# Normalized rows turned in squares by VectorE and moved by transfers, with the first pass's weight splits two chunks earlier, in a macaron block on one core

## The chip, the cores and the metric

The kernel runs on 1 core of a Trainium2 chip (trn2). The metric is the device time of one execution in microseconds (us). A matmul unit (TensorE, PE in the rows), VectorE (DVE), ScalarE (ACT) and GpSimd (POOL) each work through a list of instructions in order. SyncE (SP) only issues transfers; ScalarE and GpSimd issue some of theirs. PEld is TensorE's load of the stationary operand.

## The reference, cut to what matters

The input is 2 x 1024 tokens of 512 float32 values. Three layers follow one another, each on normalized rows:

```python
x = x + 0.5 * ffn(layernorm(x))
x = x + attention(layernorm(x))
x = x + 0.5 * ffn(layernorm(x))
```

with, for each token of `ffn` (8 groups of 352 hidden values, 64 router columns, 8 chosen):

```python
scores = softmax(x @ gate_w.T); w = top-8 of scores, scattered into 64 columns
flat = w[inv_map]; scalar = flat.sum(-1); soft = softmax(where(flat == 0, -1e9, flat))
xg = x + soft @ mask_up_w                        # for each group
y = sum over groups of scalar * (silu(xg @ Wg.T) * (xg @ Wu.T)) @ Wd.T
```

and `attention` a gated linear attention with 4 heads of 128 (keys) and 64 (values), worked in chunks of 64 tokens: projections to q, k, v, a decay and a gate, a state carried from chunk to chunk, a norm of each head's output, the gate, and a product with Wo.

## The kernel before

Four blocks of 512 tokens go through eight **phases** (p = 0 to 7). Each phase is one feed-forward layer of one block: 22 **chunks** (c), each of 128 of the 2816 hidden values. Phases 1, 2, 4 and 5 hold in addition the attention of a block (`ATT`). Every product in high precision is three TensorE products (`three`): each operand is split into a rounded part (`_hi`) and the rest (`_lo`), and `hi*hi`, `lo*hi` and `hi*lo` are added up. A split is one ScalarE copy that rounds and one VectorE subtraction.

TensorE's list for a chunk is: the gate half `main(GB)` (12 matmuls and one of `soft`), the up half `main(UB)` (12 and one), then `down` of the chunk before (12). Between these stand three **slots** per chunk, `pieces(3n)`, `pieces(3n + 1)` and `pieces(3n + 2)`, numbered k = 0 to 65 within a phase. In them all engines do, in the same numbering, what is not feed-forward matmul: `attention(t, k, q)` of this phase and `router(p, k)` for the next phase. VectorE runs slot 3n + 1 between `gate` (two products that make `act_t`) and `rest_a` (which makes `a_lo`), and slots 3n + 2 and 3n + 3 after `rest_a`; ScalarE runs slots 3n and 3n + 1 between `silu` and `round_a`, and slot 3n + 2 after it.

Before its product with weights a normalized row must lie with its features on the partitions. There are 12 normalizations of 512 rows: one for each phase's router (`LN_R`) and one for each attention (`LN_T`). Each has four tiles of 128 tokens. For a tile, VectorE writes `xn` (`norm`, line 728), TensorE turns it with four 128 x 128 transposes (`turn`, line 1063) into a bank, ScalarE rounds the bank into `x_hi` (`hi`), and VectorE writes the rest to `x_lo` (`low`). The tiles of a router sit in slots 32, 33, 35 and 36 (chunks 10 to 12), those of an attention in 7, 8, 10 and 11 (chunks 2 and 3). The router's product with `gate_s` is slot 38 (lines 1083 and 1084); the attention's first product is slot 13. `W0` and `W1` are the two banks that the slots share.

The weights of a chunk (`wt`, 1152 KB, line 272, and `dt`, 512 KB, line 281) are loaded by SP in order, `load_w(p, c)` and then `load_d(p, c - 1)`, into one of two halves. `load_w` of chunk c waits until the up half of chunk c - 2 is done (`u_ok`) and is needed by `main(GB)` of chunk c.

In phase 0 (the **first pass**) the weights arrive unsplit. ScalarE's `gu_hi(c + 1)` and VectorE's `gu_lo(c + 1)` split those of the next chunk at the head of chunk c, ahead of `silu` and `gate`; TensorE's `masked(c + 1)` (lines 1251 and 1252) behind the up half of chunk c needs them.

Of the kernel before, what the change touches and what calls it, by code (L numbers as in the profile page):

```python
# [33 lines left out]
NCK = NB // CK  # L34
EPS = 1e-5
# [27 lines left out]
def build(nc, x, wgu, wdn, wat, w_gate, w_mup, w_gk1, w_gk2, bgk, wnorm, inv, c_id, c_mask, c_reset, c_iota, c_rank, out):  # L63
    with ExitStack() as ctx:
# [14 lines left out]
        x_hi = sb("x_hi", [P, 2, KC, NB], F32R)  # L79
        x_lo = sb("x_lo", [P, 2, KC, NB], F32R)  # L80
        softT = sb("softT", [P, 2, 2, NB], F32R)
        s_bc = sb("s_bc", [P, 2, NB])
        a_hi = sb("a_hi", [P, 2, NB], F32R)
        a_lo = sb("a_lo", [P, 2, NB], F32R)
# [56 lines left out]
        xn = o_all[:].rearrange("p (a b) c -> p a (b c)", a=2)  # L141
        tb_flat = tb[:].rearrange("p a b -> p (a b)")
# [6 lines left out]
        zmin, spl = tb[:, 0:4, :], b_all  # L149

# [10 lines left out]
        def first_w(c):  # L161
# [27 lines left out]
        stats_ok, mv_ok, ve_ok, rstd_ok, xn_ok, xT_ok, x_hi_ok, x_lo_ok = (  # L189
            sem(n) for n in ("stats_ok", "mv_ok", "ve_ok", "rstd_ok", "xn_ok", "xT_ok", "x_hi_ok", "x_lo_ok"))  # L190
# [30 lines left out]
        def tr_bank(p, i):  # L221
            return YB[i] if p == 0 else W1
# [29 lines left out]
        def _(sp):  # L252
# [29 lines left out]

            for i in range(NT):
                sp.dma_start(xr(0)[:, i, :], x_t[0][:, i, :]).then_inc(ld_x0[i], 16)
# [5 lines left out]
            raw_gate_up(2)  # L290
            for c in range(2, CH):
# [126 lines left out]
        def _(act):  # L418
# [17 lines left out]
            def t_hi(t, s):  # L436
# [11 lines left out]
                elif s == S_VG:  # L448
                    act.wait_ge(k_mm, t * H)
# [10 lines left out]
            def hi(r, i, s, b):  # L460
                act.wait_ge(xT_ok, r * NT + i + 1)
                copy(x_hi[:, s, :, cols(i)], b[:].rearrange("p (k c) -> p k c", k=KC)).then_inc(x_hi_ok, 1)

            def router(p, k):
                r = LN_R[p]
                if k in (32, 33, 35, 36):
                    i = (32, 33, 35, 36).index(k)
                    if i == 0 and p:

                        wait(act, u_ok, (p - 1) * CH)  # L470
                        if p - 1 in ATT:
                            act.wait_ge(k_mm, (ATT[p - 1] + 1) * H)
                    hi(r, i, p % 2, tr_bank(p, i))
# [35 lines left out]
            def attention(t, k, q):  # L509
# [57 lines left out]
                if k in (40, 46, 52, 58):  # L567
                    h = (k - 40) // 6
                    act.wait_ge(o_ok, t * H + h + 1)
                    if h == 0:  # L570

                        act.wait_ge(xT_ok, (LN_R[q + 1] + 1) * NT)
# [3 lines left out]
                elif k in (61, 62, 63, 64):  # L576
                    i = k - 61
                    act.wait_ge(ogT_ok, t * NT + i + 1)
                    wait(act, wo_ok, t * NT + i - 1)
                    copy(og[:, i % 2, 0, :, :], W1[:, 0:2 * P].rearrange("p (v c) -> p v c", v=2)).then_inc(og_hi_ok, 1)  # L580
# [39 lines left out]
            router(0, 32)  # L620
            router(0, 33)
            act.wait_ge(ld_gate, 16)
            copy(gate_s[:, :, 0:E], raw_gate).then_inc(gate_hi_ok, 1)
            router(0, 35)
            router(0, 36)
# [14 lines left out]
            gu_hi(2)  # L640
            router(0, 45)
# [9 lines left out]
            for p in range(PHASES):  # L651
                for c in range(CH):
                    n = p * CH + c
                    if p == 0 and 1 < c < CH - 1:
                        gu_hi(c + 1)
# [12 lines left out]
                    if p == 0:  # L668
                        d_hi(c)
                    pieces(3 * n + 2)  # L670

        @block.vector
        def _(dve):
# [50 lines left out]
            def norm(r, i, src):  # L724
                dve.wait_ge(mv_ok, r * NT + i + 1)
                dve.wait_ge(rstd_ok, r * NT + i + 1)
                wait(dve, xT_ok, r * NT + i - 1)
# [3 lines left out]
            def low(r, i, s, b):  # L731
                dve.wait_ge(x_hi_ok, r * NT + i + 1)
                tt(x_lo[:, s, :, cols(i)], b[:].rearrange("p (k c) -> p k c", k=KC),
                   x_hi[:, s, :, cols(i)].bitcast(F32), ALU.subtract).then_inc(x_lo_ok, 1)

            def router(p, k):
# [5 lines left out]
                if k == 28:  # L742
# [6 lines left out]
                elif k == 29:  # L749
                    stats_of(r, 2, src)  # L750
                    stats_of(r, 3, src)
                elif k == 31:
                    norm(r, 0, src)
                    norm(r, 1, src)
                elif k in (32, 33, 35, 36):
                    i = (32, 33, 35, 36).index(k)
                    low(r, i, p % 2, tr_bank(p, i))
                    if i < 2:
                        norm(r, i + 2, src)
# [103 lines left out]
            def attention(t, k, q):  # L863
# [7 lines left out]
                elif k == 5:  # L871

                    wait(dve, ogT_ok, t * NT)
                    norm(r, 0, xb)
                    norm(r, 1, xb)
                elif k in (7, 8, 10, 11):
                    i = (7, 8, 10, 11).index(k)
                    low(r, i, s, (W0, W1)[i % 2])
                    if i < 2:
                        norm(r, i + 2, xb)  # L880
# [42 lines left out]
                if k in (61, 62, 63, 64):  # L923
                    i = k - 61
# [469 lines left out]
```

## Time and profile before

| | |
|---|---|
| median of 3 runs | 1871.08 us (1869.36 to 1872.04) |
| the profiled execution's own time | 1871.53 us |
| its span, first to last instruction | 1869.8 us |
| busy: TensorE, VectorE, ScalarE, GpSimd | 99%, 45%, 28%, 8% |
| mean granted TensorE clock | 0.995 |

The profile shows one execution. Its own time is 1.7 us above its span, and 0.45 us above the median. TensorE is busy nearly throughout; what it does and where it stops are read in the order of time, since a transfer or VectorE can hold it only in some places.

### The profile page before, as it was taken

The page shows a single profiled execution, that of the slowest core. Times are in us where ns is not written, and L with a number is a line of the kernel's source. Part 1 is how long each engine was busy: PE and PEld are TensorE (multiplying, and loading weights), DVE is VectorE, ACT ScalarE, POOL GpSimd, SP SyncE. Part 2 cuts the span into 40 slices and gives each one's busy share as a digit, 9 for nine tenths or more (in the row PEclk, how much of TensorE's full clock was granted, in tenths as well). Part 3 has the DMA queues.
Part 4 walks back from the last instruction along what each step waited for, and adds up shares of the span by engine and source line. Part 5 has one row for each costly group of instructions (what it writes and reads, how often), then busy time and mean ns, then how long its engine had stood idle before and what let it go on. Part 6 is the DMA issues. An engine that isn't in the chain of part 4 may idle for free.

```text
span 1869.8 us, 22348 instructions
## 1 busy us (share of the span) xinstructions
PE 1843.0 (99%) x8608; PEld 1533.7 (82%) x8608; DVE 841.2 (45%) x1599; ACT 526.4 (28%) x802; POOL 141.3 (8%) x246
## 2 busy tenths in 40 slices
PE   7998999999999999999999999999999999999999
PEld 5887888888888888888888888888888888888887
DVE  7455553646344554323433556353654323422222
ACT  3333422533124432111211533123532111311111
POOL 1131110010000100000010010000000000000000
PEclk9998999999999999999999999999999999999999
DMA  5985855545464455376655555455445466656664
GB/s 196 345 290 192 302 191 174 189 152 183 147 212 159 149 178 201 109 255 231 211 173 194 189 190 173 163 186 174 149 174 183 135 234 214 211 165 247 217 237 172
DMA packets 90345, 366.83 MB, mean 196 GB/s; under 512 B 11680, under 2 KB 12064, under 8 KB 69504
## 3 DMA queue, kind: packets, MB, share of 16 engines
q1 hardware_dynamic: 50064, 262.89, 40.5%
q10 hardware_dynamic: 27792, 47.20, 9.5%
q0 software_dynamic: 12384, 55.32, 7.5%
q8 instruction: 69, 1.13, 0.3%
q14 instruction: 36, 0.29, 0.0%
HBM read 323.55 MB, written 41.81 MB: 195 GB/s over the span
## 4 chain that ended last, share of the span: by engine, by line
PE 94%; DVE 3%; ACT 1%; issue 1%; DMA 1%; SPq 0%; POOL 0%; DVEq 0%; ACTq 0%
PE bank L1053 27%; PE bank L1055 27%; PE bank L1054 27%; PE bank L1266 4%; PE bank L1063 1%; PE bank L1207 1%; PE bank L1199 1%; PE bank L1206 1%; PE bank L1251 1%; PE bank L1193 1%; PE bank L1252 1%; PE bank L1083 0%; PE bank L1084 0%; PE bank L1091 0%; DMA x_res<-x 0%
## 5 line engine op out<-in xcount | busy, mean ns | idle before, releaser
L1053 PE MATMUL bank<-x_hi,wt 128*128 128x512 f32 x1328 | 524.1, 395 | 0.0
L1055 PE MATMUL bank<-x_lo,wt 128*128 128x512 f32 x1328 | 517.8, 390 | 0.0
L1054 PE MATMUL bank<-x_hi,wt 128*128 128x512 f32 x1328 | 516.9, 389 | 0.0
L675 DVE TENSOR_TENSOR act_t<-bank,sig 128x512 f32<-128x512 f32 x176 | 121.6, 691 | 571.9 <-PE bank L1266 511.7
L1055 PEld LDWEIGHTS bank<-x_lo,wt 128*128 128x128 f32 x1328 | 249.2, 188 | 53.2
L1054 PEld LDWEIGHTS bank<-x_hi,wt 128*128 128x128 f32 x1328 | 249.6, 188 | 50.2
L1053 PEld LDWEIGHTS bank<-x_hi,wt 128*128 128x128 f32 x1328 | 249.5, 188 | 49.5
L1053 PE MATMUL bank<-dt,a_hi 128*128 128x512 f32 x704 | 280.1, 398 | 0.3 <-DVE a_lo L675 0.3
L1055 PE MATMUL bank<-dt,a_hi 128*128 128x512 f32 x704 | 275.8, 392 | 0.0
L1054 PE MATMUL bank<-dt,a_lo 128*128 128x512 f32 x704 | 275.3, 391 | 0.0
L600 ACT ACTIVATE sig<-bank 128x512 f32<-128x512 f32 x176 | 105.5, 600 | 526.7 <-PE bank L1266 526.6
L420 ACT ACTIVATE a_hi<-act_t 128x512 fp32r<-128x512 f32 x176 | 111.1, 631 | 356.8 <-DVE act_t L675 349.3
L675 DVE TENSOR_TENSOR a_lo<-act_t,a_hi 128x512 fp32r<-128x512 f32 x176 | 121.4, 690 | 125.7 <-ACT a_hi L420 125.2
L1055 PEld LDWEIGHTS bank<-dt,a_hi 128*128 128x128 f32 x704 | 132.7, 188 | 28.8
L1053 PEld LDWEIGHTS bank<-dt,a_hi 128*128 128x128 f32 x704 | 133.2, 189 | 26.5 <-issue 0.7
L1054 PEld LDWEIGHTS bank<-dt,a_lo 128*128 128x128 f32 x704 | 133.0, 189 | 25.9
L1266 PE MATMUL bank<-softT,wt 128*128 128x512 f32 x352 | 134.5, 393 | 1.0 <-ACT softT L420 1.0
L675 DVE TENSOR_TENSOR act_t<-s_bc,act_t 128x512 f32<-128x512 f32 x176 | 129.2, 734 | 6.7 <-DMA s_bc<-scr_s 0.8
L1053 PE MATMUL bank<-x_hi,tw 128*128 128x512 f32 x208 | 81.6, 392 | 0.0
L1054 PE MATMUL bank<-x_hi,tw 128*128 128x512 f32 x208 | 81.4, 391 | 0.0
L1055 PE MATMUL bank<-x_lo,tw 128*128 128x512 f32 x208 | 81.3, 391 | 0.0
L1266 PEld LDWEIGHTS bank<-softT,wt 128*128 128x128 f32 x352 | 66.5, 189 | 15.0 <-issue 1.2
(178 smaller groups left out, 1690.9 us busy)
## 6 DMA issues: line engine op xcount, KB each, us to landing
wt<-scr_w SPq DMA_DIRECT2D x140, 1152.0 KB, 5.2
dt<-scr_d SPq DMA_DIRECT2D x140, 512.0 KB, 5.3
s_bc<-scr_s ACTq DMA_DIRECT2D x128, 256.0 KB, 5.2
state<-wat POOLq DMA_DIRECT2D x28, 512.0 KB, 6.2
scr_w<-wt POOLq DMA_DIRECT2D x12, 1024.0 KB, 7.6
b_all<-wgu SPq DMA_DIRECT2D x22, 512.0 KB, 6.7
scr_d<-dt POOLq DMA_DIRECT2D x22, 512.0 KB, 4.7
scr_w<-tw POOLq DMA_DIRECT2D x10, 1024.0 KB, 7.8
```

The costliest lines, as they stand in the source:

```text
L420: return nc.scalar.activation(dst, src, ACT.Copy)
L600: nc.scalar.activation(sig[:], g_bank(n)[:], ACT.Silu).then_inc(sig_ok, 1)
L675: return nc.vector.tensor_tensor(dst, a, b, op)
L1053: mm(dst, wh, xh, start=start, stop=False)
L1054: mm(dst, wl, xh, start=False, stop=False)
L1055: return mm(dst, wh, xl, start=False, stop=stop)
L1063: ins = nc.tensor.transpose(b[:, cols(k)], xn[:, i % 2, cols(k)], ident[:])
L1193: ins = mm(W0[:, cols(i)], b_all[:, h, cols(i)], q_all[:, h, cols(i)], start=True, stop=True)
L1199: ins = mm(W0[:, cols(i)], k2t[:, i, :], vtz[:, i, h, :, :], start=True, stop=True)
L1206: mm(W0[:, cols(i)], scm[:, h % 2, i, :], vtz[:, i, h, :, :], start=True, stop=False)
L1207: ins = mm(W0[:, cols(i)], q_all[:, h, cols(i)], state[:, h % 2, 2 * i:2 * i + 2, :], start=False, stop=True)
L1266: return mm(b[:], m[:, c0:c0 + P], softT[:, p % 2, c % 2, :], start=False, stop=True)
```

## The change

**Turning.** Except for the first normalization, TensorE no longer turns normalized rows. VectorE's `turn_squares` turns a tile in 32 x 32 squares into `squares` (space in `tb`), one instruction of 128 x 512. When four tiles are done (`sq_ok`), SP's `move_squares` moves them with 16 transfers of 32 partitions x 2 KB (64 KB each) into the space of `x_lo`. ScalarE then rounds two halves of 128 x 1024 into `x_hi` and VectorE writes the rests over `x_lo` (`hi`, `low`, two each in place of four). `move_squares` stands in SP's list after `load_d(p, 2)` for an attention and after `load_d(p, 11)` for a router, ahead of the next `load_w`.

**Order of tokens.** A tile of the residual holds 32 tokens of each quarter of the block, so `x_hi`, `x_lo`, `a_hi` and `a_lo` get further dimensions; TensorE's moving operand of 512 columns becomes four runs of 128, and the host reorders the rows of the input and the output.

**Slots.** The router's statistics are in 27 and 28, its norms and turns in 30 and 31 (31 and 32 where the phase holds an attention), the splits in 36 and 37. The attention's norms and turns are in 5 and 6, the splits in 10 and 11. The transposes of the gated heads (slots 61 to 64, one tile each) are done two tiles at a time in 61 and 63, and the products with Wo two tiles at a time in 64 and 65.

**First pass.** `gu_hi(c + 3)` and `gu_lo(c + 3)` stand behind the split of the down weights at the end of chunk c; chunk 3's are split before the loop.

```diff
+            def move_squares(r, s):
+                sp.wait_ge(sq_ok, r * NT)
+                for b in range(NQ):
+                    for j in range(NQ):
+                        sp.dma_start(turned(s)[cols(j, Q), b, :, :, :], squares[cols(b, Q), j, :, :, :]).then_inc(sq_in[b // 2], 16)
...
-                if c + 1 < CH:
-                    raw_gate_up(c + 1)
+                if c + 2 < CH:
+                    raw_gate_up(c + 2)
+                if c == 13:
+                    move_squares(LN_R[1], 1)
                 raw_down(c)
...
+                    if c == 3 and p in ATT:
+                        move_squares(LN_T[ATT[p]], (p + 1) % 2)
+                    if c == 12 and p + 1 < PHASES:
+                        move_squares(LN_R[p + 1], (p + 1) % 2)
...
+            def hi(r, m, s):
+                act.wait_ge(sq_in[m], 16 * 2 * NQ * r)
+                b = slice(2 * m, 2 * m + 2)
+                copy(x_hi[:, s, b, :, :, :], turned(s)[:, b, :, :, :]).then_inc(x_hi_ok, 2)
...
-                if k in (7, 8, 10, 11):
-                    i = (7, 8, 10, 11).index(k)
-                    if i == 0:
-                        act.wait_ge(u_ok, q * CH)
-                    hi(r, i, s, (W0, W1)[i % 2])
+                if k in (10, 11):
+                    hi(r, k - 10, s)
...
-                copy(a_hi[:, n % 2, :], act_t[:]).then_inc(a_hi_ok, 1)
+                copy(by_quarter(a_hi[:, n % 2, :, :, :]), in_order(act_t[:])).then_inc(a_hi_ok, 1)
...
-                    if p == 0 and 1 < c < CH - 1:
-                        gu_hi(c + 1)
                     silu(n)
...
                         d_hi(c)
+                        if 0 < c < CH - 3:
+                            gu_hi(c + 3)
...
+            def turn_squares(r, i):
+                dve.wait_ge(xn_ok, r * NT + i + 1)
+                nc.vector.transpose(squares[:, :, :, i, :].rearrange("p j k t -> p k j t"),
+                                    xn[:, i % 2, :].rearrange("p (k j t) -> p k j t", k=KC, j=NQ)).then_inc(sq_ok, 1)
...
+            def low(r, m, s):
+                dve.wait_ge(x_hi_ok, r * NT + 2 * m + 2)
+                b = slice(2 * m, 2 * m + 2)
+                tt(x_lo[:, s, b, :, :, :], turned(s)[:, b, :, :, :], x_hi[:, s, b, :, :, :].bitcast(F32),
+                   ALU.subtract).then_inc(x_lo_ok, 2)
...
+                if k in (norm_slot(p), norm_slot(p) + 1):
+                    i = 2 * (k - norm_slot(p))
...
+                    for j in (i, i + 1):
+                        norm(r, j, src)
+                        turn_squares(r, j)
+                elif k in (36, 37):
+                    low(r, k - 36, p % 2)
...
+            def xk(s, k):
+                return tuple(x[:, s, :, k, :, :].rearrange("p b i t -> p b (i t)") for x in (x_hi, x_lo))
...
-                    turn(r, i, tr_bank(p, i))
```

## Rows read from the trace of the kernel before

**Rows 1.** The page: busy us of each engine, share of the span, instructions.

```profile
PE 1843.0 (99%) x8608; PEld 1533.7 (82%) x8608; DVE 841.2 (45%) x1599; ACT 526.4 (28%) x802; POOL 141.3 (8%) x246
```

**Rows 2.** Waits of TensorE: us in total, times, longest us.

```profile
PE bank L1063 <- DVE o_all L728: 10.3, 6, 6.7
PE bank L1251 <- DVE wt L675: 6.1, 2, 3.3
PE bank L1251 <- DVE tw L675: 2.2, 2, 1.4
```

**Rows 3.** Timeline of SP: start us, us; issues of `load_w` and `load_d`.

```profile
529.06 0.32 SPq L281 DMA_DIRECT2D dt<-scr_d  x1
...
534.95 0.32 SPq L272 DMA_DIRECT2D wt<-scr_w  x1
...
544.54 0.32 SPq L272 DMA_DIRECT2D wt<-scr_w  x1
...
800.39 0.32 SPq L272 DMA_DIRECT2D wt<-scr_w  x1
...
809.00 0.32 SPq L272 DMA_DIRECT2D wt<-scr_w  x1
```

**Rows 4.** The chain that ended last, phase 1, chunk 10: a turn.

```profile
393.66 0.44 PE bank L1063 x4
```

**Rows 5.** Windows of the first pass: busy us by engine, granted clock, DMA share.

```profile
142.70:149.00 6.30, 6.30 (x20) 5.34 (x21) 3.37 (x6) 1.68 (x3) 1.60 (x3) 0.53 0.85 286
...
159.00:162.20 3.20, 3.19 (x12) 2.90 (x13) 2.30 (x5) 1.22 (x3) 1.07 (x2) 0.50 0.62 175
```

**Rows 6.** Timeline of the first pass, chunk 11: VectorE, TensorE.

```profile
140.37 0.69 DVE L675 TENSOR_TENSOR x_lo<-bank,x_hi 128x512 fp32r<-128x512 f32 x1 [5.47 <-ACT x_hi L420]
...
141.43 1.22 DVE L675 TENSOR_TENSOR wt<-b_all,wt 128x1024 fp32r<-128x1024 f32 x1
...
142.70 0.58 PE L1251 MATMUL bank<-wt,og 128*128 128x256 f32 x1 [3.26 <-DVE wt L675]
```

**Rows 7.** Groups by form, VectorE: busy us, mean ns of one.

```profile
L728 DVE TENSOR_SCALAR o_all<-x_res,mv,rstd 128x512 f32<-128x512 f32 x44 | 22.9, 540 | 0.1
...
L675 DVE TENSOR_TENSOR x_lo<-bank,x_hi 128x512 fp32r<-128x512 f32 x48 | 33.1, 689 | 58.4 <-ACT x_hi L420 58.4
...
L675 DVE TENSOR_TENSOR tw<-state,tw 128x1024 fp32r<-128x1024 f32 x28 | 34.2, 1220 | 30.8 <-ACT tw L420 30.8
```

**Rows 8.** Timeline of phase 2, chunks 1 to 4: VectorE, TensorE.

```profile
529.42 1.00 DVE L728 TENSOR_SCALAR o_all<-x_res,mv,rstd 128x512 f32<-128x512 f32 x2
...
547.91 0.48 PE L1053 MATMUL bank<-x_hi,wt 128*128 128x512 f32 x1
```

**Rows 9.** Timeline of SP and of ScalarE's queue: runs of issues.

```profile
0.80 1.81 SPq L284 DMA_DIRECT2D x_res<-x  x4
...
1698.26 0.80 ACTq L595 DMA_DIRECT2D s_bc<-scr_s  x2
...
536.42 2.54 ACTq L595 DMA_DIRECT2D s_bc<-scr_s  x2
```

**Rows 10.** Transfers by line: count, KB each, median us from issue to landing.

```profile
wt<-scr_w SPq DMA_DIRECT2D x140, 1152.0 KB, 5.2
...
s_bc<-scr_s ACTq DMA_DIRECT2D x32, 64.0 KB, 5.0
...
out<-x_res SPq DMA_DIRECT2D x4, 256.0 KB, 2.1
```

**Rows 11.** Timeline of phase 1, chunks 10 to 12: VectorE, ScalarE, TensorE.

```profile
388.47 1.00 DVE L728 TENSOR_SCALAR o_all<-x_res,mv,rstd 128x512 f32<-128x512 f32 x2
...
389.16 0.63 PE L1063 MATMUL bank<-ident,o_all 128*128 128x128 f32 x4 [0.46 <-DVE o_all L728]
...
403.28 0.60 ACT L600 ACTIVATE sig<-bank 128x512 f32<-128x512 f32 x1 [2.40 <-PE bank L1266]
...
411.41 0.48 PE L1083 MATMUL bank<-x_hi,gate_s 128*128 128x512 f32 x1
```

More of the change, by code:

```diff
@@ L219, in xr, with turned, by_quarter, in_order @@
             return x_res[:, b % 3, :, :]
-        def tr_bank(p, i):
-            return YB[i] if p == 0 else W1
+        def turned(s):
+            return x_lo[:, s, :, :, :, :].bitcast(F32)
+        def by_quarter(a):
+            return a.rearrange("p i b t -> p b i t")
+        def in_order(a):
+            return a.rearrange("p (b i t) -> p b i t", b=NQ, i=NT)
+        def norm_slot(p):
+            return 31 if p - 1 in ATT else 30
         def router_src(p):
@@ L871, in attention @@
                 elif k == 5:
[L873 to L880, printed above, removed]
+                    wait(dve, ogT_ok, 2 * t)
+                    dve.wait_ge(u_ok, q * CH)
+                    dve.wait_ge(routeT_ok, 2 * (q + 1))
+                if k in (5, 6):
+                    for i in (2 * k - 10, 2 * k - 9):
+                        norm(r, i, xb)
+                        turn_squares(r, i)
+                if k in (10, 11):
+                    low(r, k - 10, s)
                 if k in (13, 14, 15, 16):
@@ L1022, in _ @@
             gu_lo(2)
+            gu_lo(3)
             for p in range(PHASES):
@@ L1025, in _ @@
                     n = p * CH + c
-                    if p == 0 and 1 < c < CH - 1:
-                        gu_lo(c + 1)
                     gate(n)
@@ L1042, in _ @@
                         d_lo(c)
+                        if 0 < c < CH - 3:
+                            gu_lo(c + 3)
                     pieces(3 * n + 2)
@@ L1055, in three, with xtile, first_turn @@
                 return mm(dst, wh, xl, start=False, stop=stop)
-            def xk(s, k, c=slice(0, NB)):
-                return x_hi[:, s, k, c], x_lo[:, s, k, c]
-            def turn(r, i, b):
-                pe.wait_ge(xn_ok, r * NT + i + 1)
+            def xk(s, k):
+                return tuple(x[:, s, :, k, :, :].rearrange("p b i t -> p b (i t)") for x in (x_hi, x_lo))
+            def xtile(s, k, b):
+                return tuple(x[:, s, b, k, :, :].rearrange("p i t -> p (i t)") for x in (x_hi, x_lo))
+            def first_turn(i):
+                pe.wait_ge(xn_ok, i + 1)
                 for k in range(KC):
-                    ins = nc.tensor.transpose(b[:, cols(k)], xn[:, i % 2, cols(k)], ident[:])
+                    ins = nc.tensor.transpose(YB[i][:, cols(k)], xn[:, i % 2, cols(k)], ident[:])
                 ins.then_inc(xT_ok, 1)
@@ L1150, in attention @@
                     for kk in range(KC):
-                        mm(W1[:], k1_s[:, kk, :], x_hi[:, s, kk, :], start=(kk == 0), stop=False)
-                        ins = mm(W1[:], k1_s[:, kk, :], x_lo[:, s, kk, :], start=False, stop=(kk == KC - 1))
+                        x_h, x_l = xk(s, kk)
+                        mm(W1[:], k1_s[:, kk, :], x_h, start=(kk == 0), stop=False)
+                        ins = mm(W1[:], k1_s[:, kk, :], x_l, start=False, stop=(kk == KC - 1))
                     ins.then_inc(z1_ok, 1)
@@ L1223, in attention @@
-                if k in (61, 62, 63, 64):
-                    i = k - 61
+                        pe.wait_ge(t_lo_ok, t * SLABS + S_WO + 1)
+                    for i in (2 * k - 128, 2 * k - 127):
+                        if i > 1:
+                            pe.wait_ge(x2_ok, t * NT + i - 1)
+                        w = tw[:, (t * SLABS + S_WO) % 2, :].rearrange("p (a v c) -> p a v c", a=2, v=2)
+                        for v in range(2):
+                            g = [ogT(t)[:, m, v, i, :, :].rearrange("p b t -> p (b t)") for m in range(2)]
+                            ins = three((W0, W1)[i % 2][:], g, (w[:, 0, v, :], w[:, 1, v, :]), v == 0, v == 1)
+                        ins.then_inc(wo_ok, 1)
@@ L1285, in down @@
                 for t in range(NT):
-                    ins = three(YB[t][:], (a_hi[:, n % 2, cols(t)], a_lo[:, n % 2, cols(t)]), (w[:, 0:D], w[:, D:2 * D]), i == 0, i == CH - 1)
+                    ins = three(YB[t][:], tuple(a[:, n % 2, t, :, :].rearrange("p b t -> p (b t)") for a in (a_hi, a_lo)), (w[:, 0:D], w[:, D:2 * D]), i == 0, i == CH - 1)
                     if i == CH - 1 and t + 1 < NT:
@@ L1291, in _ @@
             pe.wait_ge(ld_id, 16)
-            for k in range(32, 37):
-                router(0, k)
+            for i in range(NT):
+                first_turn(i)
             pe.wait_ge(gate_ok, 1)
```

181 lines of the change are left out of this document (84 added, 97 removed).

## The prediction

> **What bounds the kernel now.** I read the page first: TensorE is busy for 1843.0 of 1869.8 us [rows 1], so only two things shorten the kernel, work taken off TensorE and its stops. The work in question is 192 transposes of normalized rows (12 normalizations of 16), of which the first 16 stay. The waits show its stops [rows 2]: on the norm before a transpose (6 times; the longest, 6.7 us, is the start of the kernel and stays) and on the split weights of the first pass (4 times, 8.3 us). The timelines give the prices, and what stands ahead of what.
>
> **Transposes off TensorE: -20.9 us.** 11 normalizations x 4 tiles x 4 = 176 transposes go, 44 turns of four. A busy sum misprices them, since they overlap and the matmul behind starts late; I price by distances. Two chunks of phase 3 without a turn are 8.61 us apart, and two of phase 2 with two turns between them 9.59 [rows 3]: 0.49 us for a turn. In the chain the turns in the chunks beside the attention's own small products take 0.44 [rows 4]. So 28 turns (16 of attentions, 12 of routers outside attention phases) at 0.49 and 16 at 0.45: 13.7 + 7.2 = 20.9 (19.4 to 21.6 by one price for all).
>
> **The wait before one turn of each attention phase: -2.6 us.** In phase 1 TensorE idles 0.46 us for the norm ahead of the turn at 389.16, which then itself takes 0.63 [rows 11]; less the 0.44 counted above this is 0.65 us, and the other attention phases repeat it: four times: -2.6.
>
> **First pass: -13.3 us.** In chunk 11 VectorE's `x_lo` waits for ScalarE's `x_hi`, which stands behind `silu`; `gu_lo`, which TensorE needs, stands behind it on VectorE, and TensorE stops for 3.26 us [rows 6]. The next chunk repeats it. After the change the splits stand at the end of a chunk and are needed over two chunks later, so nothing of 10 us can reach TensorE: the 8.3 us of [rows 2] go, with some 0.5 for the restarts. After each of the two long stops the granted clock is 0.53 over 6.3 us and 0.50 over 3.2, against 1.00 around [rows 5], that is the level of 1.2 GHz for 6.3 x 0.94 + 3.2 = 9.1 us, in which half as much was done: 4.5 us come back. Together 13.3. The cover is two chunks, over 17 us; if it went, all 13 would return. Chunk 3's split, moved before the loop, takes 1.2 us on VectorE where it waited for the first `s_bc`: nothing.
>
> **What VectorE gets.** A turn of 128 x 512 is not in this trace. From below it costs what the norm costs, 0.54 us; from above twice the sum that reads a bank, or as much as 1024 columns, 1.22 [rows 7]. I take 0.66, near the other one-pass instructions of 512 columns (0.54 to 0.69). With the norm (0.57 with its hand-over) a tile is 1.16 to 1.2 us, four 4.8. Two splits of 1024 (1.22 each) replace four of 0.69: -0.3. VectorE has over half its time free, so only places matter. The Trainium skill, page "VectorE: DVE Perf Modes", section "The three transpose paths", gives 311 ns for 128 columns in two-byte data, and says that only 32 x 32 blocks are turned; four of these would be an estimate of 1.24 us, the upper end here, and put the sum at the third rival's. No row of this trace shows the instruction.
>
> **SP's queue, attention: +1.3 us each.** Here the change adds a wait with something behind it. VectorE starts the norms of an attention at 529.42 [rows 8]; with 4.8 us and 0.1 for the signal SP is released at 534.3. Then 16 issues. Four plain issues took 1.81 us, 0.45 each; two for part of the partitions 0.80; in a busy moment two took 2.54 [rows 9]. I take 0.48, 7.7 us, to 542.0. Behind them stands `load_w(4)`, which was issued at 534.95 [rows 3]. Landing 5.2 us later [rows 10], it is there at 547.3. TensorE started that chunk at 547.91 [rows 8] behind four turns that are now gone (-1.96): it wants it at 546.0. So it stops for 1.3 us, 5.2 in four phases. At 0.40 for an issue it would not stop. The bounds: 0 to 5.6 (a turn of 1.22 adds 2.2, issues of 0.61 add 2.1).
>
> **Router in an attention phase: +0.2 us each.** The norms start at 388.47 [rows 11]; with `rest_a` between the two slots the squares are ready at 394.0, issued by 401.7, landed by 403.8 to 406.7 (2.1 to 5.0 us [rows 10]). `silu` of chunk 12 was at 403.28 [rows 11] and comes 2.0 earlier (the wait of 0.65 and three turns); ScalarE's second split stands behind the copies of the attention's scores in slot 37, by my estimate 406.4 to 407.5, and VectorE's rest ends at 408.8. TensorE wants slot 38 at 411.41 less 2.5 (a fourth turn), 408.9. It stops for 0.2, with landings late 1.5: 0.8 us in four phases. `load_w(13)`, issued at 401.7, lands at 406.9 and is wanted at 410.9. Outside attention phases the squares are ready two chunks early; the two splits around `gate` leave slot 38 about 0.1 us late, three times: 0.3.
>
> **At nothing.** The tail of the attention: with two tiles, ScalarE's and VectorE's two operations each of 256 columns (under 0.69 [rows 7]) need, by my estimate, 2.3 us behind slot 63, and TensorE's up half covers 13 x 8.61 / 38 = 2.95 [rows 3]. The runs of 32 in `a_hi` and the four runs of 128 in the moving operand: the trace has no such matmul, its runs of 128 in VectorE's writes cost no more (0.69 [rows 7]); a nanosecond for each of 6000 would be 6 us.
>
> **Sum.** -20.9 - 2.6 - 13.3 = -36.8; +5.2 + 0.8 + 0.3 = +6.3; -30.5. Against the profiled execution's own 1871.5 that is 1841.0, and the median of the runs stands 0.45 lower: 1840.6, **1841**.
>
> **Rivals.**
> 1. Nothing stops TensorE: issues of 0.40 or less. Then 1871.1 - 36.8 + 1.1 = 1835. For it speaks that transfers within the memory are short; against it that the plainest run was at 0.45. Chance 0.14.
> 2. The first pass keeps its stops, at another place (raw weights or stores late, now that TensorE is faster): 1841 + 13 = 1854. Its DMA share is 0.85 after the stop [rows 5]. Chance 0.05.
> 3. The turn costs 1.22 us. SP is released 2.2 us later, the stop at the start of an attention is 3.5 us, long enough for the lower clock as after the stops of 3 us in the first pass [rows 5] (1.5 more), and slot 38 is about 1 us late: 4 x 6 = 24 in place of 6.3, 1859. Chance 0.12.
> 4. The other side: SP's issues back up. One ScalarE run took 2.54 for two [rows 9]. If each of the 16 took 0.95 us, `load_w(4)` would be issued 7.5 us later still: a stop of 8.8 and 1.5 for the clock, and slot 38 and `load_w(13)` 3 to 5 us late, 4 x 14 = 56 against 36.8: 1890. It decides from about 0.75 us for an issue. Against it: the squares are ready 5.2 us after `load_d(2)` was issued at 529.06 [rows 3], when the queue should be empty. Chance 0.07. The Trainium skill, page "DMA: Bandwidth & Descriptors", section "Bandwidth", has 64 KB transfers at 0.95 us, bound by their descriptors; one behind another they would give this rival's time. The rows here have no transfer between two places in the core's memory.
> 5. The moving operand in four runs slows each matmul by a few ns: 2 ns x 6000 = 12 us, 1853; from 5 ns there is no gain. No row speaks for it. Chance 0.05.
>
> **How the numbers follow.** The forecast keeps 0.57, with its own range of 1836 to 1849 (the stop of an attention at 0 to 3 us). 8 in 10 is reached from 1834 to 1858, which takes in rivals 1, 2 and part of 5 and touches 3. Faster by over 0.2% (3.7 us, about what a measurement of this kernel tells from no change) is all but rival 4 and half of 5: 0.90; within it 0.03; slower 0.07.
>
> **What the profile after would show.** Right: 16 transposes in line `turn`'s place and TensorE 8432 matmuls; no wait of TensorE on split weights and a clock of 1.00 to 256 us; the VectorE turn near 0.66 us; 176 issues of 64 KB near 0.48; four waits of `main(GB)` of chunk 4 on `wt`, 1.3 us each; chunks of 8.61 us where there were turns. Wrong: waits of 3 us or more at chunk 4 or slot 38, matmuls further apart than 0.227 us, or stops in the first pass.

## The result, and the profile after

The change makes the kernel slower: 1887.62 us median (1886.73 to 1887.87, 4 runs) against 1871.56 for the kernel before beside it, a ratio of 1.0086 [1.0069, 1.0104]. The forecast was 1841, so 46.6 us have to be explained. The forecast named the side that came true, rival 4, at a chance of 0.07.

The page after, its totals, then the group of the squares among its transfers:

```profile
PE 1828.4 (97%) x8432; PEld 1520.0 (81%) x8432; DVE 872.1 (46%) x1621; ACT 521.4 (28%) x780; POOL 142.3 (8%) x246
...
PE 86%; DVE 5%; SPq 4%; DMA 3%; issue 1%; ACT 1%; POOL 0%; DVEq 0%; ACTq 0%
...
x_lo<-tb SPq DMA_DIRECT2D x176, 64.0 KB, 2.4
```

Against [rows 1] TensorE has 176 instructions less and 14.6 us less busy time, in a span 15.1 us longer: it stands still for longer. The second line is the share of each engine in the chain that ended last; SP's queue and the transfers now hold 7% of it, where they held 1% before.

Waits of TensorE, which answer to [rows 2] (us in total, times, longest):

```profile
PE bank L1111 <- DMA wt<-scr_w: 33.2, 5, 8.6
PE bank L1124 <- DVE o_all L764: 8.4, 2, 6.7
PE bank L1140 <- DVE x_lo L710: 7.7, 3, 5.8
```

The waits on split weights are gone, and those on the norm are at the start of the kernel only. New are five waits on `wt`, a load that SP issues, and one of 5.8 us for `x_lo` at slot 38. Four of the five on `wt` stand at chunk 4 of an attention phase: 6.8, 8.5, 6.8 and 8.6 us. The one of phase 2, on TensorE's and SP's timelines (start, us):

```profile
542.32 0.39 PE L1113 MATMUL bank<-dt,a_hi 128*128 128x512 f32 x1
551.19 0.79 PE L1111 MATMUL bank<-x_hi,wt 128*128 128x512 f32 x1 [8.48 <-DMA wt<-scr_w]
...
531.18 10.02 SPq L313 DMA_DIRECT2D x_lo<-tb  x16
541.24 0.58 SPq L298 DMA_DIRECT2D wt<-scr_w  x1
541.87 0.57 SPq L307 DMA_DIRECT2D dt<-scr_d  x1
542.48 0.43 SPq L298 DMA_DIRECT2D wt<-scr_w  x1
542.96 1.58 SPq L307 DMA_DIRECT2D dt<-scr_d  x1
```

The 16 issues take 10.02 us, 0.63 each. SP ran idle up to 531.18, waiting for the squares. `load_w(4)` goes out only at 541.24, and TensorE had nothing left to do at 542.7. Four loads then leave within 1.7 us, where [rows 3] has the two `load_w` among them 9.6 us apart. `load_w(4)` landed in 9.9 us; the row of that one issue, in the kernel after and, for the same chunk, in the kernel before:

```profile
wt<-scr_w SPq DMA_DIRECT2D x1, 1152.0 KB, 9.9
```

```profile
wt<-scr_w SPq DMA_DIRECT2D x1, 1152.0 KB, 7.8
```

The second line was there to be read before the change. The forecast took the median of 140 loads, 5.2 [rows 10], for a load that already took 7.8. Phase 2 is the worst of four: in phases 1, 2, 4 and 5 `load_w(4)` landed in 7.2, 9.9, 6.7 and 9.4 us, 8.3 on the mean, against 6.8, 7.8, 7.8 and 7.3 before the change, 7.4 on the mean.

What follows a stop, in windows of the kernel after (busy us of PE, PEld, DVE, ACT, POOL; then the granted clock, the DMA share, GB/s):

```profile
551.20:554.20 3.00, 3.00 (x7) 2.42 (x8) 0.00 (x0) 0.00 (x0) 0.00 (x0) 0.50 0.89 365
554.20:557.20 3.00, 3.00 (x13) 2.44 (x13) 0.00 (x0) 0.60 (x1) 0.00 (x0) 0.93 0.16 62
```

TensorE had been still for 8.5 us and worked the next 3.4 us at the level of 1.2 GHz: 1.5 us more in the first window, and 0.2 in the one behind. The same holds for all six stops that are new with the change (five on `wt`, and slot 38 below): the work at the low level behind them lasted 2.9 to 5.3 us, 21.5 in all. In the first pass SP's queue looks worse still, and slot 38 waits for it:

```profile
135.31 16.48 SPq L313 DMA_DIRECT2D x_lo<-tb  x16
151.83 0.58 SPq L287 DMA_DIRECT2D k_all<-wdn  x1
...
155.82 0.77 PE L1140 MATMUL bank<-x_hi,gate_s 128*128 128x512 f32 x1 [5.84 <-DVE x_lo L710]
```

So the 46.6 us, from these rows: the waits on `wt` at chunk 4 of four phases are 33.2 - 2.6 = 30.6 us (the fifth, 2.6, is `load_w(13)` of phase 4), 25.4 more than the 5.2 foreseen; the fifth 2.6; slot 38 of the first pass 5.8; the low clock behind the six stops 10.7, an estimate from 1.7 for the 3.4 us of phase 2. The 1.1 foreseen at slot 38 outside the first pass came to 0.3: -0.8. Together 43.7. Of the 2.9 us that are left, the first pass's own gain, which the first experiment finds 2.0 short of the forecast, can be the larger part; the rest I cannot place.

### The profile page after: what moved, and what is told of

Its sections match the earlier page's. It is cut to its first block, busy times and chain, and to the rows that moved or that the text cites. A ratio compares the mean times of both kernels' runs of the same rounds, so it can differ in the third digit from the quotient of the medians.

```text
span 1884.9 us, 22151 instructions
## 1 busy us (share of the span) xinstructions
PE 1828.4 (97%) x8432; PEld 1520.0 (81%) x8432; DVE 872.1 (46%) x1621; ACT 521.4 (28%) x780; POOL 142.3 (8%) x246
## 4 chain that ended last, share of the span: by engine, by line
PE 86%; DVE 5%; SPq 4%; DMA 3%; issue 1%; ACT 1%; POOL 0%; DVEq 0%; ACTq 0%
PE bank L1111 25%; PE bank L1113 25%; PE bank L1112 25%; SPq L313 4%; PE bank L1317 4%; DMA wt<-scr_w 2%; DVE tb L769 1%; PE bank L1257 1%; PE bank L1256 1%; DVE o_all L764 1%; PE bank L1243 1%; PE bank L1249 1%; DVE act_t L710 1%; PE bank L1140 1%; PE bank L1302 0%
## 5 line engine op out<-in xcount | busy, mean ns | idle before, releaser
L1111 PE MATMUL bank<-x_hi,wt 128*128 128x512 f32 x1328 | 526.2, 396 | 33.2 <-DMA wt<-scr_w 33.2
L1317 PEld LDWEIGHTS bank<-softT,wt 128*128 128x128 f32 x352 | 66.7, 190 | 15.1 <-issue 1.2
```

The source lines that it names most:

```text
L1111: mm(dst, wh, xh, start=start, stop=False)
L1317: return mm(b[:], m[:, c0:c0 + P], softT[:, p % 2, c % 2, :], start=False, stop=True)
```

## The experiments

All kernels were timed beside the kernel before. The reading at the start: 16 issues in series on SP, ahead of a weight load, cost the time (theory). Against it stood the bytes, and VectorE's turn.

**The first pass alone.** The kernel before, with the splits of the first pass moved and nothing else.

```diff
+            raw_gate_up(3)
...
-                if c + 1 < CH:
-                    raw_gate_up(c + 1)
+                if c + 2 < CH:
+                    raw_gate_up(c + 2)
...
+                        if 0 < c < CH - 3:
+                            gu_hi(c + 3)
```

> The kernel before with one part of the change alone: the first pass splits its gate and up weights three chunks ahead. TensorE turns the rows as before. The prediction priced this part at -13.3 us. Theory (this part kept its promise and the loss lies in the squares): 1858 us, 1855 to 1861, and no stop of TensorE for a split weight in chunks 11 to 15 of the first pass. Rival (the first pass keeps stops, its gain is small): 1866 or more.

Measured: 1860.0 us (1859.3 to 1860.5), ratio 0.9939 [0.9921, 0.9957]. Against the kernel before beside it this is -11.3 of the -13.3. The waits of TensorE hold no split weight any more; the norm and the start are left:

```profile
PE bank L1066 <- DVE o_all L730: 10.7, 7, 6.6
PE bank L1111 <- DVE tb L811: 2.0, 1, 2.0
PE bank L1086 <- DVE x_lo L677: 1.5, 1, 1.5
```

This term of the sum kept its promise within 2 us. The loss lies in the squares.

**Loads ahead of squares.**

```diff
                     if c > 1:
                         load_w(p, c)
+                    if c == 4 and p in ATT:
+                        move_squares(LN_T[ATT[p]], (p + 1) % 2)
+                    if c == 13 and p in ATT:
+                        move_squares(LN_R[p + 1], (p + 1) % 2)
                     if c > 2:
                         load_d(p, c - 1)
-                    if c == 3 and p in ATT:
-                        move_squares(LN_T[ATT[p]], (p + 1) % 2)
-                    if c == 12 and p + 1 < PHASES:
+                    if c == 12 and p + 1 < PHASES and p not in ATT:
                         move_squares(LN_R[p + 1], (p + 1) % 2)
```

> The changed kernel with the 16 square transfers of the attention phases issued by SP behind load_w(4) and ahead of load_d(3), and those of the router in the same phases behind load_w(13). Nothing else is moved, and the same bytes move. Theory (16 issues of 0.63 us stand ahead of load_w(4) on SP's queue, and the loads behind them go out in a bunch): the four stops of 6.9 to 8.75 us at chunk 4 go with the lower clock behind them, and the load of chunk 13 of phase 4 comes in time: 1887.6 - 31 - 6 - 3 = about 1848 us, 1843 to 1855; the stop of 6 us in the first pass stays. Rival 1 (the squares' bytes hold up the weights, whatever the order of issue): 1875 or more. Rival 2 (VectorE's turn comes late): no change, 1887.

Measured: 1855.59 us (1852.7 to 1858.6), 0.9915 [0.9894, 0.9937]. The same transfers in another order are worth 32 us, and turn the loss into a gain. It came out just above the theory's upper edge, because the squares, in turn, come late. Waits of TensorE:

```profile
PE bank L1142 <- DVE x_lo L712: 13.4, 6, 5.8
PE bank L1126 <- DVE o_all L766: 8.3, 3, 6.5
PE bank L1113 <- DVE x_lo L712: 3.3, 3, 2.0
```

No wait on `wt` is left. Of the 13.4 us at slot 38, 1.5 are the kernel's start, 5.8 the first pass and 6.2 the four attention phases; 3.3 are the attention's first product.

**Two issues in the place of sixteen.**

```diff
-                for b in range(NQ):
-                    for j in range(NQ):
-                        sp.dma_start(turned(s)[cols(j, Q), b, :, :, :], squares[cols(b, Q), j, :, :, :]).then_inc(sq_in[b // 2], 16)
+                for m in range(2):
+                    h = slice(2 * m, 2 * m + 2)
+                    sp.dma_start(turned(s)[:, h, :, :, :], squares[:, h, :, :, :]).then_inc(sq_in[m], 16)
```

> The changed kernel with the squares moved by 2 transfers of 128 partitions and 512 KB in the place of 16 of 64 KB. It leaves out the exchange between blocks of 32 partitions, so the rows are not in order; the bytes, the place on SP's queue and all that waits are the same. Theory (the number of issues is what costs): all stops at chunk 4 and the one of 6 us in the first pass go, 1836 us, 1832 to 1843, which is near the forecast's rival without stops. Rival 1 (the bytes on the DMA engines hold up the weights): the second half of each stop, about 4.7 of 8.6 us, stays: four of those with the lower clock behind them are 20 to 25 us, 1857 to 1862. Rival 2 (VectorE's turn comes late): 1887.

Measured: 1837.31 us (1836.9 to 1837.7), 0.9818 [0.98, 0.9835]. The bytes and the place in the queue are those of the change, and 50.3 us are gone. Its waits of TensorE, then SP's timeline at chunk 4 of phase 2:

```profile
PE bank L1124 <- DVE o_all L764: 8.9, 3, 6.6
PE bank L1140 <- DVE x_lo L710: 3.4, 2, 1.9
```

```profile
516.99 1.16 SPq L313 DMA_DIRECT2D x_lo<-tb  x2
518.19 0.92 SPq L298 DMA_DIRECT2D wt<-scr_w  x1
519.94 0.33 SPq L307 DMA_DIRECT2D dt<-scr_d  x1
```

`load_w(4)` landed here in 9.2 us, hardly earlier after its issue than the 9.9 after the change, and TensorE did not wait: what matters is when it is issued. This kernel also prices the rest of the change: it is the forecast's rival 1 (nothing stops TensorE, 1835), missed by 2.

**Half the bytes.** The column blocks of each square transfer were cut to two of four (`part`), but for the first group.

```diff
+                part = slice(0, KC) if r == LN_R[1] else slice(0, KC // 2)
...
-                        sp.dma_start(turned(s)[cols(j, Q), b, :, :, :], squares[cols(b, Q), j, :, :, :])
+                        sp.dma_start(turned(s)[cols(j, Q), b, part, :, :], squares[cols(b, Q), j, part, :, :])
```

> The changed kernel with the same 16 issues in each of 10 of its 11 groups, each moving half of its bytes (two of the four column blocks; the other two keep older values, so the rows are not right; the first group is whole). Theory (the issues on SP's queue cost, not the bytes): 1884 to 1888 us. Rival (the bytes on the DMA engines delay the landing of load_w(4)): up to half of the 4.7 us by which it lands later than elsewhere, four times, is 9 us and more with the clock: 1874 to 1879.

Measured: 1886.81 us (1885.1 to 1889.8), 1.0085 [1.0061, 1.0109]: no change against the changed kernel. SP's timeline in phase 2:

```profile
532.44 10.06 SPq L314 DMA_DIRECT2D x_lo<-tb  x16
542.54 0.58 SPq L298 DMA_DIRECT2D wt<-scr_w  x1
```

Half the bytes take the same 10.06 us to issue. The bytes are out.

**Twice the issues.**

```diff
+                        for h in (slice(0, KC // 2), slice(KC // 2, KC)):
+                            sp.dma_start(turned(s)[cols(j, Q), b, h, :, :], squares[cols(b, Q), j, h, :, :]).then_inc(sq_in[b // 2], 16)
```

> The changed kernel with 32 transfers of 32 KB in the place of 16 of 64 KB in each of the 11 groups; the same bytes, all of the computation. Theory (issues in series on SP at about 0.63 us each, with nothing of slack left): 16 more are 10 us more for each attention group (four times 10), about 8 more for slot 38 or load_w(13) of each attention phase (four times 8), 16 in the first pass, something in the three other phases: 1887.6 + 90 = about 1975 us, 1950 to 2000. Rival (the time is in the bytes): 1888 to 1895.

Measured: 1995.88 us (1993.3 to 1996.6), 1.067 [1.0653, 1.0687]. The 176 further issues cost 108.3 us, 0.62 each, and SP's timeline shows where:

```profile
562.49 20.39 SPq L314 DMA_DIRECT2D x_lo<-tb  x32
582.92 0.58 SPq L298 DMA_DIRECT2D wt<-scr_w  x1
```

32 issues of 32 KB take 0.64 us each, as 16 of 64 KB did. That 0.62 is an average over all groups, with the low clock behind longer stops in it. At chunk 4 the 16 further issues hold `load_w(4)` back by 10.0 us on the mean of the four phases, and the stop grows by 7.1 only, since the load now lands sooner; its row in phase 2:

```profile
wt<-scr_w SPq DMA_DIRECT2D x1, 1152.0 KB, 5.3
```

In the four phases it took 5.3 to 5.6 us, behind 32 squares. So the squares ahead of it are not what made it land late; the open point at the end comes back to this. The waits on `wt` stayed at five and those for `x_lo` went from 7.7 us to this:

```profile
PE bank L1141 <- DVE x_lo L711: 72.2, 8, 15.0
PE bank L1112 <- DMA wt<-scr_w: 61.0, 5, 15.1
```

**`load_w(4)` alone.**

```diff
+                    if c == 4 and p in ATT:
+                        sp.wait_ge(w_in[chunk(p * CH + 4) % 2], 16 * ((p - 1) * (HALF - 1) + 2))
                     if c > 2:
                         load_d(p, c - 1)
```

> The changed kernel with one wait more on SP: in the attention phases load_d(3) is issued only when load_w(4) has landed. The 16 issues stay where they are. The stop at chunk 4 was 8.6 us in phase 2, of which I put 4.7 to the landing of load_w(4) in 9.9 us and not 5.2. Theory (the landing is late because four loads go out within 2 us behind the squares): load_w(4) lands in 5.0 to 6.5 us, each of the four stops is 3.5 to 4.5 us shorter, and load_d(3), wanted half a chunk later, is still in time: 1887.6 - 16 = about 1872 us, 1868 to 1878. Rival (the squares' own transfers or the queue hold it up, or load_d(3) is late in its stead): 1885 or more.

Measured: 1887.96 us (1884.3 to 1889.0), 1.0092 [1.0076, 1.0108]. My theory falls here. SP's timeline shows that the load had the queue for itself:

```profile
532.61 10.03 SPq L313 DMA_DIRECT2D x_lo<-tb  x16
542.68 0.58 SPq L298 DMA_DIRECT2D wt<-scr_w  x1
551.31 0.33 SPq L307 DMA_DIRECT2D dt<-scr_d  x1
```

It landed in 8.6 us all the same. The bunch of loads behind it accounts for about 1.3 of the 9.9 in phase 2, for 0.2 on the mean of the four phases (8.1 against 8.3), and for none of the time.

**The squares on GpSimd's queue.** The same `move_squares` in GpSimd's list: after the attention's second weight slab, after `rstd_of` for a router, and in the first pass behind `store_m(12)`.

```diff
+                    if n == S_VG + 1:
+                        move_squares(LN_T[t], (q + 1) % 2)
...
                     rstd_of(LN_R[q + 1])
+                    move_squares(LN_R[q + 1], (q + 1) % 2)
...
                 store_m(c)
+                if c == 12:
+                    move_squares(LN_R[1], 1)
```

> The changed kernel with all 11 groups of squares issued by GpSimd (POOL) in the place of SP: the same 16 transfers of 64 KB each, so the same number, bytes and shape, but no weight load behind them. Theory (it is SP's queue and its loads that wait): the stops at chunk 4 and at chunk 13 of phase 4 go; what GpSimd's own issues cost is open, at about 1 us each 16 us for a group, with slot 13 and slot 38 in time or up to 5 us late, 8 times: 1840 to 1875. Rival (16 small transfers disturb the weight loads on the DMA engines, whoever issues them): the stops at chunk 4 of more than 4 us stay, 1875 or more.

Measured: 1877.25 us (1874.5 to 1878.4), 1.0035 [1.0021, 1.0048]. Waits of TensorE, then GpSimd's timeline in phase 2:

```profile
PE bank L1140 <- DVE x_lo L710: 28.7, 8, 8.4
...
PE bank L1111 <- DVE x_lo L710: 1.5, 2, 1.2
```

```profile
528.92 2.48 POOL L388 DMA_DIRECT2D x_lo<-tb  x5 [4.88 <-DVE tb L769]
532.84 5.38 POOL L388 DMA_DIRECT2D x_lo<-tb  x11 [1.44 <-issue]
```

The waits on `wt` are gone, though the same 16 transfers pass over the DMA engines: it was the queue. The new cost is at slot 38, ahead of all seven routers whose squares are moved, since GpSimd's 16 take 9.3 us with a pause of 1.4 and land in 6.2 us at the median.

**`load_w(4)` when the squares have landed.** The kernel just shown, with a wait of SP for the whole group ahead of `load_w(4)`; one run.

```diff
+                    if c == 4 and p in ATT:
+                        sp.wait_ge(sq_in[1], 16 * 2 * NQ * LN_T[ATT[p]])
                     if c > 1:
                         load_w(p, c)
```

> The kernel with all squares issued by GpSimd, with one wait more: in the attention phases SP issues load_w(4) only when all 16 squares of the group have landed. It separates what stands in load_w(4)'s own queue from what else moves at that time. In the changed kernel the load took 8.6 us to its last packet and its first packet started 3.1 us after its issue, elsewhere 4.7 and 0.95. Theory (two parts: about 2.2 us wait in the queue behind the last squares, the rest is shared time on the DMA engines with the attention's own weights): here the first packet starts 0.95 us after the issue, and the load ends 5 to 7 us after it. Rival (the moment alone is busy, the queue adds nothing): first packet after 2 to 3 us, end after 8 to 9.

Measured: 1907.64 us, one run. In phase 2 the load was issued at 546.83 and landed in 7.4 us; its first packet started 2.7 us after the issue, in the other phases 1.7 to 2.5. The theory's 0.95 us did not come in any phase. The landings were 6.8, 7.4, 6.5 and 8.5 us in phases 1, 2, 4 and 5: two in the theory's 5 to 7, one in the rival's 8 to 9, one between. With no square left in flight the first packet was still late, so the queue behind the squares is not what delays it. What does stays open (below).

**Through the device's main memory.** Four transfers write the squares, two read them back in order.

```diff
+                for b in range(NQ):
+                    sp.dma_start(scr_x[s, :, :, b, :].rearrange("j q e -> q j e"),
+                                 squares[cols(b, Q), :, :, :, :].rearrange("p j k i t -> p j (k i t)")).then_inc(sq_out, 16)
+            def fetch_squares(r, s):
+                sp.wait_ge(sq_out, 16 * NQ * r)
+                for m in range(2):
+                    h = slice(2 * m, 2 * m + 2)
+                    sp.dma_start(turned(s)[:, h, :, :, :].rearrange("p b k i t -> p b (k i t)"),
+                                 scr_x[s, :, :, h, :].rearrange("j q b e -> (j q) b e")).then_inc(sq_in[m], 16)
```

> The changed kernel with the exchange made through the device's main memory: 4 transfers write the squares of 32 partitions each, and 2 read them back in order, 6 issues in the place of 16, with load_w between the writes and the reads; in the first pass the writes stand ahead of raw_gate_up(15). All of the computation. Theory (what costs is the number of issues ahead of a weight load): 4 issues are 2.4 us, so load_w(4) goes out in time or under 1 us late, and no stop above 1 us is left in an attention phase; squares land 8 to 10 us after they are ready, where over 14 us are there: 1836 us, 1833 to 1844. Rival (a round trip through memory under a busy DMA takes 15 us and more): slot 13 and slot 38 are late by several us, 1855 or more.

Measured: 1895.69 us (1892.2 to 1899.9), 1.0144 [1.0117, 1.0171]. The rival won. SP's timeline in phase 2, then the waits of TensorE:

```profile
533.38 2.85 SPq L315 DMA_DIRECT2D scr_x<-tb  x4
536.27 1.33 SPq L300 DMA_DIRECT2D wt<-scr_w  x1
541.11 0.81 SPq L322 DMA_DIRECT2D x_lo<-scr_x  x2
```

```profile
PE bank L1156 <- DVE x_lo L726: 25.1, 8, 9.4
PE bank L1265 <- ACT scm L475: 9.1, 4, 4.7
...
PE bank L1127 <- DVE x_lo L726: 4.7, 4, 2.2
```

The weights are in time, but for 1.2 us in phase 4; two landings follow one another: 7.7 us from the first write to the reads, then 6.5 at the median of the two reads and 7.8 for the second. `x_lo` is late at slot 38 (8 waits, one of them at the kernel's start) and at the attention's first product (4), and ScalarE, which waits for it at slot 36, brings its copies `scm` late too.

**Two queues.** SP issues the transfers with j = 0 and 1, GpSimd those with 2 and 3, in the places of the two kernels above.

```diff
-                    for j in range(NQ):
+                    for j in (0, 1):
...
+            def move_squares(r, s):
+                pool.wait_ge(sq_ok, r * NT)
+                for b in range(NQ):
+                    for j in (2, 3):
```

> The changed kernel with each group of 16 square transfers split over two queues: SP issues 8 of them (in the place where it issued 16) and GpSimd the other 8 at the same time. All of the computation, the same bytes and number. Theory (what costs is the issues in series on one queue, ahead of a load): SP's 8 issues take 5 us, load_w(4) goes out 5 us earlier and the stops of 6.9 to 8.75 us at chunk 4 shrink to 2 to 4 us; the stop of 6 us in the first pass and the small ones at slot 38 go: 1887.6 - 18 - 7 - 4 = about 1855 us, 1846 to 1862. Rival (the two queues share one limit, the transfers are no faster together): 1875 or more.

Measured: 1846.4 us (1844.1 to 1847.6), 0.9869 [0.9854, 0.9883]. SP's timeline in phase 2:

```profile
523.42 5.54 SPq L314 DMA_DIRECT2D x_lo<-tb  x8
529.00 0.59 SPq L299 DMA_DIRECT2D wt<-scr_w  x1
...
532.26 0.32 SPq L299 DMA_DIRECT2D wt<-scr_w  x1
...
540.87 0.32 SPq L299 DMA_DIRECT2D wt<-scr_w  x1
```

Eight issues, 5.5 us, and `load_w(4)` lands in 5.4 us; the waits on `wt` are 0.4 us in all. The theory had left 2 to 4 us for each; but it had the stop of the first pass go, and that one stood at 6.8 us. The last two rows are also the price of a turn: they stand 8.61 us apart with no turn between them, where two turns made it 9.59 [rows 3].

**Two queues, loads first.** The same, with the order of SP from the second experiment.

> The same split over two queues, and on SP load_w(4) and load_w(13) of the attention phases ahead of its half of the squares. All of the computation. Theory (nothing stands ahead of the weights any more, and the squares are landed half as late): of the 18 us by which the kernel with the loads first stood above the one with two transfers, those at slot 38 and at slot 13 and the stop in the first pass go: 1840 us, 1836 to 1846. Rival (GpSimd's half is issued no earlier than the loads-first half, and slot 38 keeps its stops of 1.4 to 2.1 us): 1848 to 1853.

Measured: 1860.26 us (1852.8 to 1867.3, 8 runs), 0.9948 [0.993, 0.9966]. Neither theory nor rival. With eight issues, the squares no longer hold up `load_w`, so putting them behind it only makes them late: `x_lo` costs 14.1 us of waits at slot 38, where the kernel before this had 8.3. Its runs also scatter over 14 us, and the profiled one (1852.8) is the fastest of them; the scatter I don't explain.

**Two queues, GpSimd's half earlier in the first pass.**

```diff
                 store_m(c)
-                if c == 12:
+                if c == 11:
                     move_squares(LN_R[1], 1)
```

> The kernel with the squares split over two queues, and GpSimd's half of the group in the first pass moved ahead of store_d(11), store_w(13) and store_m(12), behind which it stood: there it was issued at 142.09, 11 us after its rows were ready, and TensorE stopped for 7.0 us at slot 38. All of the computation. Theory (that stop was the place in GpSimd's queue): GpSimd's half goes out at 134.6, the stop shrinks to 1 us or less: 1846.4 - 7.5 = about 1839 us, 1836 to 1842, which is the forecast for the change (1841) within its own error, now with all parts. Rival (SP's own 8 issues, 1.27 us each there, set the stop): 1844 to 1847.

Measured: 1841.72 us (1840.9 to 1843.0), 0.9849 [0.9835, 0.9862], the best complete version: 28.5 us below the kernel before. The time lies in the theory's range (1836 to 1842), but its reason did not hold: the wait at slot 38 shrank from 6.8 to 5.1 us and not to 1 or less, so the stop was not GpSimd's place alone. GpSimd's eight transfers had landed by 144.9, SP's last at 150.4: it is SP's half that sets the stop now, as the rival had it. SP's timeline:

```profile
133.21 14.21 SPq L314 DMA_DIRECT2D x_lo<-tb  x8
147.46 0.67 SPq L288 DMA_DIRECT2D k_all<-wdn  x1
```

Eight issues take 14.2 us here, 1.78 each: in the first pass the stores of the split weights (1 MB each, landing in 9.4 us there) are under way at the same time. That they slow the issues is my reading; no run took them away.

## Why the prediction was wrong, point by point

- **The step that failed** is "SP's queue, attention: +1.3 us each". It was put together from an issue of 0.48 us and a landing of 5.2, and measured 7.7 on the mean of the four (30.6 / 4), plus the low clock behind it. Both of its terms were too small, by about as much: on the mean of the four phases the 16 issues took 10.8 us and not 7.7, which makes 3.1, and `load_w(4)` landed in 8.3 and not 5.2, another 3.1; the turn, 0.71 and not 0.66, with its hand-overs makes 0.5. With the 1.3 foreseen that is 8.0, against 7.7. In phase 2 alone the issues make 2.3 (0.63 each) and the landing 4.7. That the issues on SP's queue cost the time, and not the bytes, the turn or the bunch behind, was shown by the kernels with two issues (-50.3 us), with half the bytes (no change), with 32 (+108.3) and with another order (-32). Of the second 3.1 us, 2.2 were there before the change (a mean landing of 7.4).
- The issue's price came from plain issues of 0.40 and 0.45 [rows 9], while the same group held a pair at 2.54 / 2. The bound of 0.61 that the text gave was nearly right. The upper bound for the stop, 5.6, was still too low, because it held the landing at the median of all loads. The row of the one load concerned, 7.8, was in the trace.
- **Rival 4** had the right mechanism and side with a wrong threshold: it was to decide from 0.75 us for an issue, and it decided at 0.63 to 0.72, since the landing was late as well. Its argument against ("the queue should be empty") was of no help: SP had issued nothing for 5 us before the squares, and their issues still went out 0.63 us apart from the second on. The 0.95 us that the Trainium skill has for a transfer of 64 KB (page "DMA: Bandwidth & Descriptors", section "Bandwidth") is the time for which the DMA engines are busy with a load from main memory that GpSimd issues, and not the price of an issue, for which the rival took it; and the page calls transfers under 64 KB bound by their descriptors, where the prediction says it of 64 KB. SP's issues took 0.63 to 0.72 here, and 1.03 in the first pass, and transfers of half the bytes 0.64.
- **First pass: -13.3.** Right in mechanism: -11.3 measured alone. But inside the whole change the squares of its router, costed like the others outside attention phases at 0.1 us, met 16.48 us of issues and stopped TensorE for 5.8. The forecast named no price for an issue under the first pass's DMA load, though [rows 5] showed a share of 0.85.
- **Router in an attention phase: +0.2.** Right for slot 38; the 2.6 us of phase 4 were missed. There a load of `x_res` stood between the squares and `load_w(13)`, which costs 0.5 us of issue; the larger part is that `load_w(13)` landed in 8.5 us, where it took 5.4 to 6.1 in the other three attention phases.
- **Transposes -20.9 and the wait -2.6.** Right: the kernel with two issues has all parts but the exchange and is at 1837.3, where the sum without stops gave 1835, and a stop of 1.9 in the first pass covers most of that difference. No run has these two terms alone: they are what is left of its gain; that is 34.0 less the 11.3 of the first pass, 22.7, and 24.6 with the stop of 1.9 taken out, against 20.9 + 2.6 = 23.5.
- **Rival 3**, a turn of 1.22 us, is out. The group of the turn, by form:

```profile
L769 DVE STREAM_TRANSPOSE tb<-o_all 128x512 f32<-128x512 f32 x44 | 31.3, 712 | 1.5
```

- The 0.712 us stand against the estimate of 1.24 from the Trainium skill's 311 ns for 128 columns (page "VectorE: DVE Perf Modes", section "The three transpose paths"); the measurement decides. **Rival 5**, a slower moving operand, is out: matmuls in four runs of 128 start 0.227 us apart as before. **Rival 2** is out by the first experiment; the stop that did appear in the first pass belongs to the squares.
- **Open:** why `load_w(4)` lands late. In phase 2 it took 7.8 us before the change, 9.9 after, 9.2 with two issues, 8.6 alone, 7.4 with the squares landed, 5.4 with two queues and 5.3 behind 32 issues. The traces narrow it down. In ten kernels the attention's own slab (`wat`, 512 KB, on GpSimd's queue) is still in flight when `load_w(4)` goes out, and the 40 loads of their attention phases took 6.2 to 9.9 us. In three (two queues, two queues early, 32 issues) it has landed or is issued 2.7 us or more later, and the 12 loads took 5.3 to 5.9. The rows of GpSimd's queue (q0) and SP's (q1) in the 2 us behind the issue, kernel after, phase 2:

```profile
q0 software_dynamic: 111, 0.45, 77.5%
q1 hardware_dynamic: 48, 0.07, 8.8%
```

The slab moves most of the bytes there, and the first packet of `load_w(4)` starts 3.1 us after its issue; with 32 issues nothing moves on q0, and it starts after 1.2. That is an association and not an experiment: no run moved the slab by itself, the scalars of the chunk (`s_bc`, 256 KB) mostly go out at the same time, and the kernel through main memory took 8.4 to 9.4 without the slab, with its own writes under way.

## What to carry to other kernels

An exchange in many small transfers is paid by their number on the queue that issues them, and the bill goes to the load that stands behind. Before such a group is put ahead of a load, take the landing of that very load from the trace and not the median of its line, and take the price of an issue from a stretch with the same DMA load. Where a queue is too short for a group, a second queue beside it did more here (1846.4, and 1841.7 with the better place in the first pass) than another order (1855.6), all on GpSimd's queue (1877.3) or fewer, larger steps with a round trip (1895.7).

## What the runs showed of the hardware

- A transfer between partitions of the core's memory costs SP 0.63 to 0.72 us of issue by the mean of a group of 16 in the kernel after, and 0.63 to 0.66 with half the bytes in groups of 32, both outside the first pass. Beside the stores of the first pass it was 1.03 in the kernel after and 1.78 in the last one. GpSimd's went at 0.49 us in runs of eight (3.95 us).
- Two queues with eight issues each overlap: in phase 2 the group was issued in 5.5 us in place of 10.0, at equal bytes.
- VectorE turns a 128 x 512 tile of float32 in squares of 32 in 0.71 us, against 0.54 for the one-pass norm of the same size.
- In the kernel after, each of the six new stops of TensorE (2.6 to 8.6 us) was followed by work at the clock of 0.50, 2.9 to 5.3 us of it, and the length did not follow that of the stop: 3.2 us after a stop of 2.6, 5.3 after 6.8, 3.4 after 8.5. A stop of 2.8 us in the kernel with GpSimd's queue (at 1379.8) was followed by 3 us at 1.00.
- A load of 1152 KB from main memory landed in 5.3 to 5.9 us where no slab of 512 KB was in flight on GpSimd's queue at its issue, and in 6.2 to 9.9 where one was (`load_w(4)`, 52 loads in 13 kernels; the kernel through main memory, 8.4 to 9.4, left out).
